# A four-layer fused token model on one Trainium2 core: the last mixture writes the output from its own blocks, and the linear attention is written out

## The reference, cut to what matters

```python
# L2 attention (no softmax), xn = layernorm(x), one batch b of 113 tokens at a time
theta = xn @ W_theta.T            # (113, 64)
phi   = xn @ W_phi.T              # (113, 64)
g     = xn @ W_g.T                # (113, 256)
x     = x + theta @ (phi.T @ g) / 16   # a 64 x 256 memory for each batch
...
# L3 feed-forward: 8 experts, one pick for each token
p      = softmax(xn @ w_router); e = argmax(p)
y      = relu(xn @ w1[e] + b1[e]) @ w2[e] + b2[e]
x      = x + p[e] * y             # the output
```

## Time and profile before

| | us |
|---|---|
| median of 3 runs | 1459.32 (1455.14 to 1463.46) |
| the profiled execution | 1472.0 |
| its span, first to last instruction | 1470.3 |
| mean granted TensorE clock | 0.846 of full |
| busy: PE, DVE, ACT, POOL | 1047.1, 1028.9, 751.0, 519.4 |

### The profile page before, as it was taken

How to read it: one execution, slowest core, us unless ns; L and a number is a source line. 1 busy time by engine, 2 the same in 40 slices (tenths; PEclk the granted TensorE clock), 3 DMA queues, 4 the chain that set the end, 5 groups by cost and what they waited for, 6 DMA issues and landing times. The chain is left out here.

```text
span 1470.3 us, 28385 instructions
## 1 busy us (share of the span) xinstructions
PE 1047.1 (71%) x9099; PEld 705.2 (48%) x9099; DVE 1028.9 (70%) x2229; ACT 751.0 (51%) x1493; POOL 519.4 (35%) x620
## 2 busy tenths in 40 slices
PE   3558877753699986766658867266589995389991
PEld 2322322232356553554446744144466663388880
DVE  5779999987256445567967654788758887646552
ACT  5557777742476653125437632244358885244440
POOL 0249888850444427501011100000136665122204
PEclk9669999975799998788978978589669997589996
DMA  5001111000465644202000000000013331112214
GB/s 227 15 22 37 43 43 43 29 26 26 129 165 149 165 137 135 70 6 86 1 0 1 1 1 0 0 0 0 19 69 107 114 117 57 47 51 66 66 48 122
DMA packets 50687, 89.84 MB, mean 61 GB/s; under 512 B 8555, under 2 KB 34867, under 8 KB 49715
## 3 DMA queue, kind: packets, MB, share of 16 engines
q1 hardware_dynamic: 43360, 67.20, 14.3%
q0 software_dynamic: 6912, 18.88, 4.8%
q10 hardware_dynamic: 288, 2.10, 0.5%
HBM read 72.11 MB, written 16.04 MB: 60 GB/s over the span
## 5 line engine op out<-in xcount | busy, mean ns | idle before, releaser
L1133 POOL TENSOR_TENSOR scan_ch<-scan_hs,scan_ct 128x452 f32<-128x452 f32 x128 | 143.6, 1143 | 40.7 <-DVE scan_hs L1247 36.9
L1158 PE MATMUL scan_py<-scan_ch,ident 128*128 128x452 f32 x256 | 131.0, 601 | 37.7 <-POOL scan_ch L1133 28.0
L1247 DVE TENSOR_TENSOR_SCAN scan_hs<-scan_abar,scan_bx 128x452 f32<-128x452 f32 x128 | 133.2, 1084 | 1.2 <-DVE scan_bx L1239 0.6
L2224 DVE TENSOR_SCALAR m3x_a<-m3x_ph,m3x_b 128x128 f32<-128x128 f32 x184 | 49.7, 343 | 68.4 <-ACT m3x_ah L2202 66.2
L1158 PEld LDWEIGHTS scan_py<-scan_ch,ident 128*128 128x128 f32 x256 | 40.6, 193 | 107.0 <-POOL scan_ch L1133 100.2
L1207 ACT ACTIVATE scan_abar<-ssm_dt,ssm_a 128x448 f32<-128x448 f32 x128 | 79.8, 634 | 13.2 <-DVE scan_hs L1247 12.7
L2202 ACT ACTIVATE m3x_ah<-m3x_ph,m3x_b 128x128 f16<-128x128 f32 x184 | 50.1, 383 | 65.0 <-PE m3x_ph L463 60.9
L3146 POOL TENSOR_TENSOR mha_prob_lo<-mha_prob,mha_prob_hi 113x452 f16<-113x452 f32 x64 | 65.8, 1051 | 38.2 <-ACT mha_prob_hi L3315 38.2
L461 PE MATMUL m3x_ph<-m3x_xb,m_w_hi 128*128 128x128 f16 x368 | 74.3, 223 | 2.6 <-DVE m3x_al L2235 2.2
L462 PE MATMUL m3x_ph<-m3x_xb,m_w_hi 128*128 128x128 f16 x368 | 74.4, 224 | 0.0
L463 PE MATMUL m3x_ph<-m3x_xb,m_w_lo 128*128 128x128 f16 x368 | 74.2, 223 | 0.0
(11 more groups left out here) (697 smaller groups left out, 3808.2 us busy)
## 6 DMA issues: line engine op xcount, KB each, us to landing
mha_wbuf<-m3w SPq DMA_DIRECT2D x32, 512.0 KB, 3.3
scan_piece<-m0w SPq DMA_DIRECT2D x30, 256.0 KB, 2.7
m0x_b<-m0b SPq DMA_DIRECT2D x57, 128.0 KB
m_out<-m0x_yo SPq DMA_DIRECT2D x57, 128.0 KB
tok_wbuf<-m0w SPq DMA_DIRECT2D x5, 768.0 KB, 9.4
m3x_b<-m3b SPq DMA_DIRECT2D x23, 128.0 KB, 3.1
m_out<-m3x_yo SPq DMA_DIRECT2D x23, 128.0 KB
m_rows<-m0r_parts SPq DMA_DIRECT2D x4, 448.0 KB
```

The source lines that it names most:

```text
L1133: pool.tensor_tensor(ch[r][:], hs[r][:], ct[n % 2][:], ALU.mult).then_inc(weighed, 1)
L1158: pe.matmul(py[c][:, 0:GT], core.ident[:], ch[u % R][:], start=n == 0, stop=n == NS - 1).then_inc(summed, 1)
L1247: dve.tensor_tensor_scan(hs[u % R][:], abar[c][:, 0:GT], bx[u % R][:], 0.0, ALU.mult, ALU.add).then_inc(scanned, 1)
```

## The change

Three parts.

1. **Linear attention written out.** The hardware loop over groups goes; PE, ACT and DVE get one straight sequence over the 16 batches, theta has two buffers in SBUF and in PSUM, and the next group's theta stands inside the current group. Batches are projected two ahead. The arithmetic is the same.
2. **The router keeps what the blocks need.** The route stage of the second mixture stores `core.h` to a DRAM table `m_res` of 1808 rows of 257 words, and later the router's weight of each token as the 257th word of its row. Token numbers are counted from 1, so that an empty lane shows as 0: `m.dest` holds the output row of each lane, or a number far out of bounds for an empty one; `m.ids` holds the row to read, as before.
3. **Blocks finish their rows.** In the expert stage POOL gathers the 128 rows of `m_res` for each block (`kept`), DVE computes `ys = yo * weight + h`, and POOL scatters `ys` into the output by an indirect DMA that skips rows out of bounds. SP no longer stores `yo`. The combine stage is gone. POOL's sequence is written out.

```diff
@@ stage_route @@
+                if m.one:
+                    kept = m.res.rearrange("(b t) n -> t b n", t=L)
+                    for r, n in ROWS:
+                        sp.dma_start(kept[r:r + n, :, 0:D], core.h[r:r + n]).then_inc(kept_stored, 16)
                 for q in range(NG):
                     sp.wait_ge(row_lo, q + 1)
...
+                if m.one:
+                    sp.wait_ge(weight_made, 1)
+                    for r, n in ROWS:
+                        sp.dma_start(kept[r:r + n, :, D:D + 1], m.weight[r:r + n], allow_slow_non_contiguous=True).then_inc(kept_stored, 16)
+                    sp.wait_ge(kept_stored, 16 * 2 * len(ROWS))
...
-                ch.step(dve.tensor_copy(m.ids[:], pids[:]))
+                if m.one:
+                    ch.step(dve.tensor_scalar(empty[:], pids[:], 0.5, 8192.0, ALU.is_lt, ALU.mult))
+                    dve.scalar_tensor_tensor(m.dest[:], pids[:], -1.0, empty[:], ALU.add, ALU.add)
+                ch.step(dve.tensor_scalar(m.ids[:], pids[:], -1.0, 0.0, ALU.add, ALU.max))
@@ stage_experts, POOL @@
-                steps(pool, N - 3, step)
+                def gather_kept(n):
+                    p, before = n % 4, n // 4
+                    wait_alone(pool, core, summed[p], before)
+                    pool.indirect_dma_start(kept[p][:], None, m.res[:, :], ...
+                def scatter(n):
+                    p, before = n % 4, n // 4
+                    wait_alone(pool, core, sent[p], before * 16)
+                    pool.tensor_copy(dest[p][:], m.dest[:, n:n + 1]).then_inc(dest_ready[p], 1)
+                    wait_alone(pool, core, dest_ready[p], before + 1)
+                    wait_alone(pool, core, summed[p], before + 1)
+                    pool.indirect_dma_start(final[:, :], bass.IndirectOffsetOnAxis(ap=dest[p][:, 0:1], axis=0),
+                                            ys[p][:], None, bounds_check=T - 1, oob_is_err=False).then_inc(sent[p], 16)
+                for n in range(N):
+                    gather_kept(n)
+                    if n + 3 < N:
+                        gather(At(0, n + 3))
+                    bias(At(0, n))
+                    if n >= 3:
+                        scatter(n - 3)
                 for n in range(N - 3, N):
-                    bias(At(0, n))
+                    scatter(n)
@@ stage_experts, DVE and SP @@
+                def weigh(n):
+                    p, r = n % 2, n % 4
+                    dve.wait_ge(y_out[p], n // 2 + 1)
+                    dve.wait_ge(kept_landed[r], n // 4 * 16 + 16)
+                    need(dve, sent[r], n // 4 * 16)
+                    dve.scalar_tensor_tensor(ys[r][:], yo[p][:], kept[r][:, D:D + 1], kept[r][:, 0:D], ALU.mult,
+                                             ALU.add).then_inc(summed[r], 1)
...
-                    sp.dma_start(m.out[bass.ds(at.j * 128, 128), :], yo[p][:]).then_inc(stored[p], 16)
@@ stage_linear_attention, PE (ACT and DVE follow the same order) @@
-                with pe.Fori(0, NG) as q:
-                    ...
-                    project(0)
-                    for j in range(GB):
-                        if j + 1 < GB:
-                            project(j + 1)
-                        collect(j)
-                        if j:
-                            spread(j - 1)
-                    spread(GB - 1)
+                project(0)
+                theta(0)
+                project(1)
+                for b in range(NB):
+                    collect(b)
+                    if b % GB == 1 and b // GB + 1 < NG:
+                        theta(b // GB + 1)
+                    if b:
+                        spread(b - 1)
+                    if b + 2 < NB:
+                        project(b + 2)
+                spread(NB - 1)
```

More of the change, by code:

```diff
@@ L1297, in __init__ @@
         self.late = 10 if gelu else 0
+        self.one = picks == 1
     def buffers(self, nc, ctx, weights):
@@ L1708, in _ @@
                     for b in range(q * GB, (q + 1) * GB):
-                        ins = act.activation(numbered[:, b], block_hot[:, b], ACT.Copy, scale=token[:, b:b + 1])
+                        ins = act.activation(numbered[:, b], block_hot[:, b], ACT.Copy, scale=number[:, b:b + 1])
                     ins.then_inc(blocks_numbered, 1)
@@ L2084, in stage_experts @@
         yo, b2 = ([st.sb(f"{n}{p}", [128, D]) for p in two] for n in ("yo", "b2"))
+        ys, kept = [st.sb(f"ys{p}", [128, D]) for p in four], [st.sb(f"kept{p}", [128, D + 1]) for p in four]
+        dest = [st.sb(f"dest{p}", [128, 1], U32) for p in four]
         pt = [st.ps(f"pt{p}", [128, 1024], F16) for p in two]
@@ L2272, in _ @@
                 steps(sp, N - 2, step)
-                for n in range(N - 2, N):
-                    store(At(0, n))
-                sp.wait_ge(stored[0], 16 * ((N + 1) // 2))
-                sp.wait_ge(stored[1], 16 * (N // 2))
 class Combine:
@@ L2313, in add @@
         ins.then_inc(self.added, 1)
-def stage_combine(nc, core, m, out):
-    with Stage(nc, m.name + "c") as st:
-        combine = Combine(st, m)
-        stored = st.sem("stored")
-        rows = out.rearrange("b t d -> t b d")
-        with nc.Block() as block:
-            @block.sync
-            def _(sp):
-                for q in range(NG):
-                    sp.wait_ge(combine.added, (q + 1) * GB)
-                    for r, n in ROWS:
-                        sp.dma_start(rows[r:r + n, q * GB:(q + 1) * GB, :],
-                                     core.h[r:r + n, q * GB:(q + 1) * GB, :]).then_inc(stored, 16)
-                sp.wait_ge(stored, 16 * len(ROWS) * NG)
-            @block.gpsimd
-            def _(pool):
-                combine.gather(pool, core)
-            @block.vector
-            def _(dve):
-                for b in range(NB):
-                    combine.add(dve, core, b // GB, b % GB)
 def stage_shared(nc, core, d, m, w, middle):
@@ L2840, in _ @@
                     act.wait_ge(th_ready, q + 1)
[L2842 to L2852 removed]
+                    need(act, o_ready, (q - 1) * GB)
@@ L2854, in _ @@
+                high_gate(0)
+                high_theta(0)
+                high_gate(1)
+                for b in range(NB):
+                    high_memory(b)
+                    if b % GB == 1 and b // GB + 1 < NG:
+                        high_theta(b // GB + 1)
+                    if b + 2 < NB:
+                        high_gate(b + 2)
             @block.vector
             def _(dve):
-                def add(q, j):
-                    p = j % 2
-                    dve.wait_ge(o_ready[p], q * 2 + (j // 2 + 1))
-                    b = bass.ds(q * GB + j, 1)
-                    dve.tensor_tensor(core.h[:, b, :], po[p][:, 0:D].unsqueeze(1), core.h[:, b, :],
-                                      ALU.add).then_inc(o_free[p], 1)
@@ L2880 @@
+                low_gate(0)
+                low_theta(0)
+                low_gate(1)
+                for b in range(NB):
+                    low_memory(b)
+                    if b % GB == 1 and b // GB + 1 < NG:
+                        low_theta(b // GB + 1)
+                    if b:
+                        add(b - 1)
+                    if b + 2 < NB:
+                        low_gate(b + 2)
+                add(NB - 1)
 MAGIC = 12582912.0
```

158 lines of the change are left out of this document (86 added, 72 removed).

## The result

| | before | after |
|---|---|---|
| median of 4 runs, us | 1459.69 | 1425.22 |
| lowest to highest | 1455.14 to 1463.46 | 1424.31 to 1428.16 |
| profiled execution, its span | 1472.0, 1470.3 | 1424.37, 1422.2 |
| mean granted clock | 0.846 | 0.858 |

The ratio is 0.9762, with a 95% interval of 0.9744 to 0.9781: faster by 34.5 us. The forecast was 1419 with a range of 1408 to 1434.

What follows compares the result with a forecast made beforehand. PE bounds the experts; 29.8 us follow the last yo, and linear attention takes 52.5 with uncovered work. Profiled 1472.0 - 15.2 - 25.6 + 0.4 = 1431.6, less 12.7 for the median, gives 1419 us; range 1408 to 1434.

Steps and rivals of the forecast that it cites:

- Linear attention (gain 15.2): Linear attention: in the new order PE should be the bound, its last add ending at 902.9; gain 15.2 us, bound 7.8.
- Route (+0.4): Route stage: the stores of h and the weight words cost 0, two more DVE instructions at its tail cost 0.4 us.
- Experts, steady (0): Expert blocks: POOL's 5.26 us of work a block stays under PE's 6.36, so the added gather and scatter cost 0.
- 1.7 early: Expert blocks: the bias is ready at 1352.5 and ACT takes it at 1354.22, so it comes 1.7 us early.
- 1.1 to spare: Expert blocks: POOL's work sums to 5.26 us against 6.36 a block, so POOL keeps 1.1 us to spare.
- The evidence against it: Against POOL being held by DVE: a gather took 0.97 us while DVE ran eight operations beside it.
- rival B: Expert blocks: POOL binds partly or the bias comes late; 1436 us if a scatter costs 2.8; chance 0.12.
- The tail (gain 25.6): Program end: without the combine stage it closes at 1444.7, 0.8 us after the last scatter lands; gain 25.6, bounds 23 to 27.
- C: Route stage: the 4-byte weight stores hold it open, +6 to +10 us, 1425 to 1429; chance 0.06.
- rival D: Linear attention: the clock stays low or its chain of waits stays as long; no gain gives 1434 us; chance 0.05.
- E: Whole kernel slower than before: a scatter costing POOL 3.8 us or more eats both gains; chance 0.03.
- Rival A: Whole kernel: the case as worked out, 1410 to 1428 us; chance 0.74.

Runs made afterwards that it cites:

- run 10: Changed kernel plus one more indirect gather in each block, into a buffer nothing reads: 1457.95 us, ratio 0.9912 to the kernel before.
- Run 3: Changed kernel with the expert stage's block closed without GpSimd's drain: 1418.83 us, ratio 0.9715 to the kernel before.
- run 6: Changed kernel with one more GpSimd drain, behind the bias of the last block: ratio 0.973 to the kernel before.
- run 9: Changed kernel without the closing drain, biases loaded four blocks ahead, last three destinations copied early, offset copies kept: ratio 0.9718 to the kernel before.
- run 2: Kernel before with kept rows, weights and scatter from the blocks, but the old linear attention: 1444.31 us, ratio 0.9892 to the kernel before.
- run 5: Changed kernel with offsets of all three indirect transfers read straight from the tables, without copies: 1443.65 us, ratio 0.9802 to the kernel before.
- run 11: Changed kernel again, unchanged, in a later set: 1433.64 us, ratio 0.9746 to the kernel before.
- run 12: Changed kernel with only the scatter's offsets read straight from the table: 1434.83 us, ratio 0.9731 to the kernel before.
- run 4: Changed kernel plus two more indirect gathers in each block, into buffers nothing reads: 1468.09 us, ratio 1.0054 to the kernel before.
- run 8: Kernel before, unchanged, profiled once more: 1473.92 us with a span of 1472.2.

## Why the prediction was right, step by step

**Linear attention (gain 15.2).** Right: 14.8 inside the profile; timed alone 16.9, with an interval from 15 to 20, of which some 2 us lie in the stages behind it. PE is the bound, the clock does not fall between groups, and the batches stand 1.86 apart as the sum of collect, spread and project had it.

**Route (+0.4).** Right: first start of the route stage to the first gather is 0.4 longer. The weight words, whose upper bound was dear, land in 3.6 us; the 1.5 to issue and 1.5 to confirm of that bound came from no row, and the issue took 1.16. The forecast took 0 between bounds of nothing and 5.8 without a row for such a transfer, so that it is right here is in part luck. The 1840 packets under 512 B show that the 1808 words went as pieces of their own. The Trainium skill ("DMA: Bandwidth & Descriptors", Rules for kernel authors) says that a last dimension that is not contiguous becomes one descriptor for each element. The trace agrees on the pieces and shows no cost in time.

**Experts, steady (0).** The cost is right, two of the reasons behind it are not. The scatter costs 1.03 us on POOL (forecast 0.97 or more). But the bias is not "1.7 early": ACT waits for it in 9 blocks, and the forecast had named just that as a sign of being wrong. And POOL does not keep "1.1 to spare": one gather of 1.25 us more costs 1.3 to 1.4 us a block (run 10), so nearly nothing was left. One block of after shows where the chain from `ys` to the bias is longer:

```profile
1345.16 0.48 DVE L2300 SCALAR_TENSOR_TENSOR m3x_ys<-m3x_yo,m3x_kept 128x256 f32<-128x256 f32 x1
1346.57 1.02 POOL L2159 DMA_INDIRECT out<-m3x_ys,m3x_dest  x1 [1.60 <-DVE m3x_ys L2300]
1349.83 1.60 POOL L2133 DMA_INDIRECT m3x_xg<-m_rows,m3x_idx  x1 [0.75 <-POOL m3x_idx L2131]
1351.43 0.20 POOL L2142 COPY m3x_b<-m_b 128x8 f32 x1
1351.75 2.17 ACT L2253 ACTIVATE m3x_ah<-m3x_ph,m3x_b 128x128 f16<-128x128 f32 x8 [3.24 <-POOL m3x_b L2142]
```

The bias is there 6.0 us after the end of `ys`, and the forecast had 4.45 (1352.5 - 1348.05). Two things were missing. The scatter starts 0.93 after `ys` ends, where the forecast had it at once, 0.08 after. And the token gather takes 1.60 and not 0.97. That is time in which POOL is held by DVE. In each of the nine blocks of after from 1305 to 1357 one POOL instruction takes longer than elsewhere, and always one that overlaps `m3x_al`. The longest, with DVE's row:

```profile
1311.45 2.02 POOL L2133 DMA_INDIRECT m3x_xg<-m_rows,m3x_idx  x1 [0.75 <-POOL m3x_idx L2131]
```

```profile
1311.40 1.23 DVE L2286 TENSOR_TENSOR m3x_al<-m3x_a,m3x_ah 128x1024 f16<-128x1024 f32 x1
```

This gather starts 0.05 us after `m3x_al` and takes 2.02 us and not 0.97. The evidence against it, was an indirect DMA beside DVE's `m3x_a`, which reads its tensor `m3x_ph` from PSUM, the memory that PE writes, and does not hold POOL; `m3x_al` reads two tensors from SBUF, and beside that one POOL is held. In the rows of before from 1300 to 1380 no gather starts while `m3x_al` runs, so that trace could not show it. The Trainium skill ("SBUF — State Buffer", "SBUF: two separate sides") says that DVE and GpSimd share a port pair as an exclusive lock: a DVE operation with two SBUF inputs, against a GpSimd operation that reads SBUF, keeps it for the whole instruction if it starts first, and the other is blocked. The trace agrees for POOL's copy in run 10: 1.22 us for 0.20, ending 0.04 us behind DVE. The gather ends 0.84 us behind it, which is most of a gather's 0.97. The blocks kept their 6.3 us all the same, since part of the late bias fell into time in which ACT was idle before too. POOL at 5.45 plus up to 1.05 was at the edge of binding, and rival B was nearer than its 0.12.

**The tail (gain 25.6).** This is the term that was mis-sized: 19.2. The forecast closed the program "0.8 later" than the last landing and gave 4.2 us from the end of the last `yo` to the end. Measured, from 1412.04: `ys` 0.53; wait for the scatter 0.88, where the forecast had none; scatter 0.98; landing and waits 1.4, forecast 1.8; then the drain 5.70, which the forecast does not have; 0.7 to the end. That is 10.2. Run 3 shows the drain's price by leaving it out, 5.7 us inside the stage, and run 6 by moving it, 5.2. The kernel before had such a drain as well, in the combine stage, but under other work (the view of that block's line):

```profile
L2322 POOLq DRAIN  x1: 4817/4817/4817, 1461.8 to 1461.8; - x1
```

It runs from 1461.8 to 1466.6, the first 2.2 us of it still behind POOL's own last two gathers, while DVE adds until 1466.5 and the last output store moves until the end. The change took that cover away: now the last work is POOL's own. The sum thus came out 6 us low, 1419 for 1425.2. The range held since it was wide enough on that side, but that width was there for rivals B and C: that it also covered a drain nobody had counted is luck.

**The rest.** The clock did not stay low in the linear attention (rival D), the small stores held nothing (C), and no scatter came near 3.8 us (E). Rival A, the case as worked out, is what happened, less the drain.

## What to carry to other kernels

When a stage at the end is removed, list what used to run beside the old end, drains and barriers among it, and price it as uncovered: the profile before showed the drain, and I did not look for it. Where every software DMA is waited for by its own semaphore, the block can be closed without GpSimd's drain (1418.8 us here, the lowest ratio of the study, with run 9 equal within noise), or the drain be put earlier under other work. And a margin on POOL is not its busy time against the period: add its waits between copy and transfer, the 0.85 to 0.93 us from the end of DVE's `ys` to the start of a scatter that waited for it, and the time that DVE's operations on two SBUF tensors hold it.

## What the runs showed of the hardware that was not expected

**A drain costs by what was issued.** Behind waits for every scatter, GpSimd's drain took 0.39 us behind 4 indirect transfers (run 6), 5.70 behind 69 (after and runs 2, 5, 11 and 12) and 7.58 behind 92 (run 10), some 0.08 us for each transfer since the drain before. The early drain of run 6 fits with 5.5 behind 65, and so does the one of the shared stage in after, behind 48 gathers: it ends 4.0 us after the last of them. Behind 23 it took 2.17 in before, 0.09 for each. One point lies far off: 2.60 us behind 115 (run 4). That outlier is unexplained. Nearly all transfers had 128 rows, so whether the price goes by transfers, by rows or by bytes is not told apart.

**Less work on POOL made PE slower** (run 5: 0.3 us a block, 6 us in all, though PE's program was the same). The effect is measured in two kernels; its cause is not. The low granted clock at the start of the stage, 0.61 in run 5 and 0.77 in the second window of runs 9 and 10, is measured in one execution each.

**The granted clock of a stage differs between executions of the same code.** Part of the shared stage, 560 to 600 us, in the profile after and in run 8:

```profile
560.00:600.00 40.00, 26.74 (x152) 16.59 (x152) 28.27 (x58) 12.31 (x24) 29.86 (x29) 0.87 0.30 90
```

```profile
560.00:600.00 40.00, 20.20 (x93) 11.67 (x91) 21.25 (x43) 8.71 (x16) 24.80 (x26) 0.70 0.28 79
```

From the first mixture's first gather to the first statistics behind the shared stage it is 267.2 us in after and 280.7 in run 8. All four kernels of the first set have 264.8 to 267.6 there, all of the later sets, on other chips, 275.8 to 281.5. That is more than several of the effects studied here, so two spans of different sets say little; a ratio to a kernel timed beside it does.
